# Group 0's FFN blocks on TensorE behind the spreads of C, its second tile's output ahead of the later gates, and its last tile's values and scale in the closing stage

## What is computed

```python
# x + xattn: hidden = ctx (4,256,128), z = layernorm(x) (4,256,256)
x = einsum(in_proj_w, hidden); xc = depthwise_conv(x, 4 taps); u = silu(xc + conv_b)
dt_lo, Bm, Cm = split(x_proj_w @ u)                    # 8, 16 and 16 rows
delta = softplus(dt_proj_w @ dt_lo + dt_proj_b); A = -exp(A_log)       # 256 x 16
state = state * exp(delta * A) + (delta * u) * B       # per token, per channel, 16 states
y = sum_over_16_states(state * C) + D * u;  y = y * silu(z)
x = x + y
# FFN on h = layernorm(x); bit_linear rounds x to 8 bits by its token's maximum and w to {-1,0,1}
gate = silu(bit_linear(h, gate_w, gate_b)); val = bit_linear(h, val_w, val_b)   # 1024 wide
x = x + bit_linear(gate * val, out_w, out_b)
```

## Time and profile before

| | |
|---|---|
| Median of 3 runs | 218.53 us (218.25 to 222.1) |
| The profiled execution | 218.7 us, of it the span from the first to the last instruction 216.8 us |
| Busy in the span | DVE 176.1 us, PE 149.0, POOL 137.5, ACT 133.4 |
| Mean granted clock of PE | 0.795 |
| The chain that ended last, by engine | DVE 22%, PE 21%, issue 8%, ACT 4%, POOL 2% |

### The profile page before, as it was taken

The page is one execution under the profiler, slowest core; times in us unless marked ns, Lnnn a source line. Parts: engine busy times, 40 slices in busy tenths (PEclk is TensorE's granted clock), DMA queues, the critical chain, the costliest instruction groups (busy, mean ns, idle before and its releaser), DMA issues.

```text
span 216.8 us, 2402 instructions
## 1 busy us (share of the span) xinstructions
PE 149.0 (69%) x706; PEld 92.4 (43%) x706; DVE 176.1 (81%) x269; ACT 133.4 (62%) x207; POOL 137.5 (63%) x134
## 2 busy tenths in 40 slices
PE   6983049871793687776107987737886478899983
PEld 5531035351451575566105444425463165335452
DVE  3787999959939969999999397996489998757771
ACT  2569656896189869761307579365975206286672
POOL 5039499997965994967849999993069004690000
PEclk9995558996555579696755587966699969999999
DMA  4994953450331110040024031322000000000002
GB/s 117 243 336 135 331 177 82 146 206 29 142 98 48 33 63 0 12 136 2 0 91 151 3 87 78 126 89 80 0 5 26 0 0 0 4 23 15 9 24 73
DMA packets 12689, 17.44 MB, mean 80 GB/s; under 512 B 3468, under 2 KB 9012, under 8 KB 12678
## 3 DMA queue, kind: packets, MB, share of 16 engines
q1 hardware_dynamic: 12678, 17.30, 24.9%
HBM read 16.11 MB, written 1.19 MB: 80 GB/s over the span
## 4 chain that ended last, share of the span: by engine, by line
DVE 22%; PE 21%; issue 8%; ACT 4%; POOL 2%; DVEq 0%; POOLq 0%
DVE state L934 4%; PE work L1275 4%; PE ysum L1189 4%; DVE wstate L944 3%; DVE gam L1015 2%; DVE xhat L849 2%; PE decay L1099 2%; DVE pool_state L934 2%; PE work L1099 2%; PE work L1282 2%; DVE wstage L1010 2%; PE work L1315 2%; PE decay L1275 1%; ACT gT L748 1%; PE cwide L1210 1%
## 5 line engine op out<-in xcount | busy, mean ns | idle before, releaser
L497 POOL TENSOR_TENSOR drive<-du,b_wide 128x1024 f32<-128x1024 f32 x31 | 73.8, 2395 | 3.1 <-DVE du L925 2.8
L679 ACT ACTIVATE decay<-delta,aneg 128x510 f32<-128x510 f32 x64 | 43.0, 685 | 29.5 <-DVE state L934 15.0
L934 DVE TENSOR_TENSOR_SCAN state<-decay,drive 128x512 f32<-128x512 f32 x44 | 52.4, 1208 | 2.7 <-ACT decay L679 2.4
L1189 PE MATMUL ysum<-ident,wstate 128*128 128x128 f32 x176 | 34.3, 343 | 9.8 <-DVE wstate L944 9.8
L1189 PEld LDWEIGHTS ysum<-ident,wstate 128*128 128x128 f32 x176 | 27.9, 180 | 18.0 <-DVE wstate L944 13.0
L944 DVE TENSOR_TENSOR wstate<-state,cwide 128x512 f32<-128x512 f32 x44 | 29.0, 662 | 7.5 <-issue 7.5
L507 POOL TENSOR_TENSOR pool_wstate<-pool_state,c_wide 128x1024 f32<-128x1024 f32 x10 | 23.6, 2361 | 13.7 <-PE ysum L1189 11.6
L1210 PE MATMUL cwide<-cparts,sel 128*128 128x512 bf16 x22 | 10.5, 476 | 26.0 <-DVE wstate L944 14.2
L934 DVE TENSOR_TENSOR_SCAN pool_state<-decay,drive 128x512 f32<-128x512 f32 x20 | 24.3, 1216 | 2.2 <-ACT decay L679 2.2
L1275 PE MATMUL work<-ternary,qT 128*128 128x512 bf16 x46 | 15.1, 416 | 3.8 <-ACT wstage L729 1.6
L1099 PE MATMUL work<-ident,wstage 128*128 128x128 f32 x80 | 12.5, 301 | 5.4 <-ACT ternary L703 2.8
(11 more groups left out here) (186 smaller groups left out, 290.5 us busy)
## 6 DMA issues: line engine op xcount, KB each, us to landing
b_wide<-bc_rows SPq DMA_DIRECT2D x16, 512.0 KB, 4.3
c_wide<-bc_rows SPq DMA_DIRECT2D x10, 256.0 KB, 3.4
x_in<-in_x SPq DMA_DIRECT2D x2, 512.0 KB, 4.0
wstage<-in_L_ffn_gate_w SPq DMA_DIRECT2D x1, 1024.0 KB, 7.6
wstage<-in_L_ffn_val_w SPq DMA_DIRECT2D x1, 1024.0 KB, 10.1
wstage<-in_L_ffn_out_w SPq DMA_DIRECT2D x1, 1024.0 KB, 8.9
ctx_in<-in_ctx SPq DMA_DIRECT2D x2, 256.0 KB, 3.7
out<-wtap SPq DMA_DIRECT2D x4, 128.0 KB, 1.7
```

Of the source, the lines that this page charges most:

```text
L497: nc.gpsimd.tensor_tensor(drive[:, m % NDR], du[:, m // NS], rows.unsqueeze(1).to_broadcast([P, EH, W]), ALU.mult).then_inc(s_drive, 1)
L679: nc.scalar.activation(v[:, :, 1:L], d[:, :, 1:L], ACT.Exp, scale=aneg[:, eh, n:n + 1]).then_inc(s_decay, 1)
L934: nc.vector.tensor_tensor_scan(dst, decay[i % ND][:], drive[:, i // EH % NDR, i % EH], 0.0, ALU.mult, ALU.add).then_inc(s_scan, 1)
L1189: last = nc.tensor.matmul(ysum[:, k, eh * P:(eh + 1) * P], lhsT=src[:, k * P:(k + 1) * P], rhs=ident[:], start=start and k % LB == 0, stop ...
```

## The change

It is made in the tables and in four places of the code. On PE, group 0's gate, val, turn and output blocks stand after other units than before; the z transposes move from unit 51 to 62. DVE and ACT follow. The output of tile 1 is formed before the gates of tiles 2 and 3. On DVE, the values and the scale of tile 3 leave the loop and come in the closing stage, behind the read of out02; ACT quantises that tile behind its gate(1, 0). POOL's scale parts for the second half of group 1 wait until tile 3's values are read. The list `scans` is written in the new order.

```diff
-PE_Z, ACT_Z, PE_ZLATE = (22, 23), (24, 25, 54, 55), 51
+PE_Z, ACT_Z, PE_ZLATE = (22, 23), (24, 25, 64, 65), 62
...
-PE_GATE, ACT_GATE = (39, 44, 51, 53), (44, 47, 56, 58)
-PE_VAL, DVE_VAL, DVE_VAL2 = (45, 48, 59, 60), (46, 48, 60, 62), (47, 49, 61, 62)
-ACT_QUANT, PE_TURN, ACT_TURN = (52, 54, 65, 68), (49, 54, 65), (53, 61, 67)
-PE_OUT, DVE_OUT = (50, 58, 67), (51, 60)
+PE_GATE, ACT_GATE = (40, 44, 56, 58), (44, 47, 58, 60)
+PE_VAL, DVE_VAL, DVE_VAL2 = (48, 50, 60, 67), (49, 51, 61), (50, 52, 62)
+ACT_QUANT, PE_TURN, ACT_TURN = (53, 55, 65), (52, 54, 65), (54, 57, 67)
+PE_OUT, DVE_OUT = (53, 55, 67), (54, 57)
...
-    scans += tile(0, 0, "val") + tile(0, 1, "val") + tile(0, 0, "turn", "out") + ["z2", "z3"]
-    scans += tile(0, 2, "gate") + tile(0, 3, "gate") + tile(0, 1, "turn", "out")
-    scans += tile(0, 2, "val") + tile(0, 3, "val") + tile(0, 2, "turn", "out")
+    scans += tile(0, 0, "val") + tile(0, 1, "val") + tile(0, 0, "turn", "out") + tile(0, 1, "turn", "out")
+    scans += tile(0, 2, "gate") + tile(0, 3, "gate") + tile(0, 2, "val") + ["z2", "z3"] + tile(0, 2, "turn", "out")
+    scans += tile(0, 3, "val")
...
                 if g:
                     wait_read(pool, "acol00")
+                if k:
+                    wait_read(pool, f"val0{GT - 1}{CH - 1}")
                 pool.wait_ge(s_tok, g + k + 1)
...
-            for i in range(ACT_QUANT[-1] + 1):
+            for i in range(ACT_TURN[-1] + 1):
                 if i < G * UNITS:
                     decays(i)
...
             for t in range(GT):
                 ffn_gate(1, t, ACT.Silu)
                 if t == 0:
+                    ffn_quantise(0, GT - 1)
                     ffn_hidden(0, GT - 1)
...
             ffn_output(0, GT - 2)
+            for c in range(CH):
+                ffn_value(0, GT - 1, c)
+            ffn_scale(0, GT - 1)
             for t in range(GT):
                 for c in range(CH):
                     ffn_value(1, t, c)
```

## The result

| | before | after |
|---|---|---|
| Median of 4 runs each | 219.63 us (218.25 to 222.1) | 227.0 us (225.83 to 227.78) |
| Ratio after / before, 95% interval | | 1.035 (1.026 to 1.045) |
| The profiled execution, and its span | 218.7, 216.8 | 226.95, 225.0 |
| Mean granted clock of PE | 0.795 | 0.780 |

The changed kernel is slower by 3.5%. The ratio compares the runs within 1.5% of the fastest of their kernel, the others being slow executions (of before here 222.1), so it is not the quotient of the medians. The next two rows are from the page of the profile of after: the busy time of each engine in the span, and the chain of work that ended last, by line.

What follows compares the result with a forecast made beforehand. DVE was taken as busiest, with PE bounding the end from 187.36. From 218.7, minus 3.4 (scans), plus 9.3 (val product) and 1.6 (turn), gave 226.2, median 226.0 us; 80% range 221.5 to 230.0.

Steps and rivals of the forecast that it cites:

- What bounds the end of the kernel: Closing stage: from 187.36, first half of group 1, PE is busy 21.27 of 21.40 us, so its delays reach the end.
- The first spread: Scans, unit 40: spread ahead of the gate block, weigh 3.1 us sooner, all of it going into waiting for POOL.
- Scan 48: Scans: ACT's block starts about 1.1 us sooner, so this scan starts at 134.7 instead of 137.34.
- waits (a) and (b): New DVE waits: 1.2 us at scan 59 (work0 held by out01), 2.7 us for decay 61 (ACT's second silu block).
- R: Start of the closing stage, 179.58 before; claimed 3.4 us sooner, bounds 0.5 to 5.5.
- Tile 3's val product: Closing stage: val031 waits for DVE's read of out02, holding up PE; delay 9.3 us, bounds 6.8 to 12.1.
- The clock term: Closing stage, PE after its stand: 5 us of half clock, costing 2.5 us of the delay.
- The turn: Closing stage: tile 3's transposition waits for ACT's quantising behind gate(1,0); 1.6 us on PE, 1.2 to 1.7.
- The one in which PE is hardly held: Rival, closing stage: out02 is read before PE reaches val031; 217.7 us, no change; chance 4%.
- The one with a cheap hold: Rival: PE is held as said, but cheaply, and the scans gain all; 221.0 us; chance 9%.
- The one in which the scans gain nothing: Rival: PE stays at half clock in the scans and gate 3 is late; 228.9 us, up to 231; chance 20%.
- The one in which the scans gain all that the two waits promise: Rival: the scans gain 7.4 us and PE is hardly held in the closing stage; 213.7 us; chance 2%.

Runs made afterwards that it cites:

- four experiments on the closing stage: Changed kernel with out02 read early, 218.48 us; or with out02 in bank 6 and a later turn, 216.49; also 14 warm-ups, 216.44; also POOL's additions later, 214.5.
- Re-ordering alone: Changed kernel with tile 3's val product, values, scale and quantising left in the scans; 218.78 us, ratio 0.997 to the kernel before.
- two experiments on out02: Changed kernel with out02 moved to bank 6, 222.88 us, ratio 1.006; or with DVE reading out02 ahead of normalising, 218.48 us, ratio 0.990.
- tail part alone: Kernel before with only tile 3's values, scale and quantising moved to the closing stage, its val product behind out02; 231.9 us, no ratio given.
- First spread alone: Kernel before with only tile 0's gate product on PE put behind the spread of unit 40; 217.22 us, ratio 0.993.

## Why the prediction was right, point by point

- **What bounds the end of the kernel.** "From 187.36 on the end of the kernel follows PE": right. In before, after and the four experiments on the closing stage in which PE's clock stays up, the time from the first half to the end is 29.3 to 31.1 us, wherever the first half lies.
- **The first spread.** Said: the weigh of unit 40 waits 0.6, then waits for POOL before scans 44 and 46, nothing won. Measured: 0.50, 1.34 and 1.71. The step held for the wait. "Buys nothing by itself" did not hold for the kernel: alone, the edit gave 0.7%, through stretches that I had taken as unchanged.
- **Scan 48, and waits (a) and (b).** Said 134.7, 1.2 and 2.7; measured 135.12, 1.19 and 2.62. All of after is 0.88 us later by scan 39 already (116.01 for 115.13), so scan 48 came some 0.5 us sooner than worked out. The wait before it, 1.55, is the shorter of its two lengths ("Re-ordering alone"): with the lower clock at that place it would have been 3.0 to 3.1, which the prediction did not see.
- **R.** Said 3.4 us sooner, with 1.2 us taken off for a low clock; measured 3.22 sooner, or 4.10 from scan 39 on. The wait for the last sum grew from 0.75 to 1.39 us: the sums stand behind the z transposes, and from 166.1 to 172.9 the granted clock was 0.50. That is a piece of the 1.2. That 3.22 lies so near to 3.4 is in part luck: the stretch that the prediction is about gained 4.10, 0.7 more than said, and the 0.88 us by which this execution was late before it took that back.
- **Tile 3's val product.** This is the step that makes the kernel slower. Said: a gap of some 5.8 us ended by the read of out02, val031 at R + 9.2, a delay of 9.3. Measured: 5.53 us ended by DVE's L1028, R + 9.21, 17.52 - 7.78 = 9.74. The two experiments on out02 show that this bank is the cause: 8.6 and 7.5 us of the delay go with it.
- **The clock term.** Said 2.5; val031 and the warm-ups took from 185.57 to 193.88, 8.31 us against 5.34 at full clock, so 3.0. That 0.5 is the miss in the delay: 5 us of half clock were taken, and 3.0 us lost stand for some 6. The choice of 5 between two rows was an estimate that no run bore out beforehand. The row that shows the level is that of 185 to 190, 0.50. The Trainium skill (TensorE: Matmul & The Clock Gate, Part 1) has the array at 1.2 GHz after idling. This trace agrees, with a granted clock of 0.50 behind the stand of 5.53 us. The same part of the Trainium skill puts the cost of ramping back at under 1% of a typical kernel's span, which would be at most 2.2 us here (an estimate). The trace shows 3.0 us, 1.3% of the span, for a single gap, and the measurement decides.
- **The turn.** Said 1.6; first half to end grew from 29.44 to 31.12, 1.7. The mechanism, ACT's quantising behind gate(1,0), is shown by the kernel that takes the turn later. Tile 3's values and scale cost nothing, as said: DVE is done with them at 190.0 and then waits 8.46 us. What the prediction did not have is that the turn's gap of 1.9 us can cost more than itself; in after it did not.
- **Sum.** -3.2 + 9.7 + 1.7 = +8.2, as the spans say (225.0 - 216.8); said were -3.4 + 9.3 + 1.6 = +7.5. The errors of +0.2, +0.4 and +0.1 have one sign, and 226.95 stands where 226.2 was worked out. By lengths from scan 39 on they have not: -0.7 in the scans, with 0.9 us from ahead of unit 39, then +0.4 and +0.1.
- **The rivals.** The one in which PE is hardly held is what happens once out02 has another bank or an early reader, and not otherwise. The one with a cheap hold fails on the clock: the hold cost 3.0 us at the lower level. The one in which the scans gain nothing fails on the 4.10 us. The one in which the scans gain all that the two waits promise is refuted by the re-ordering alone, with a ratio of 0.997.

## What to carry to other kernels

When a product is moved to a new place in a rotation of PSUM banks, look up what held its bank last, which engine reads that and behind how much other work: PE's queue stops at the first tile whose bank is not free, and everything behind it, fillers too, is late by the sum. A wait for one supplier is worth only as much as the next supplier is earlier; here two waits of 7.4 us in sum went, and five others of 1.2 to 2.6 us each, for POOL and ACT, came in their place, 8.4 us in sum. Matmuls put in to keep the clock up stood, before, where PE would have waited; when the queue ahead of them changes, as here, they turn in part from filler into cost.

## What the hardware showed

The clock did not always fall after a gap of the same length. The turn waits for 1.89 or 1.90 us in five kernels after almost the same work. In after and in the kernel with the early read the clock stays at 1.00 behind it (194 to 215 above, and 191 to 194 in the other); in the kernel with another bank and in that without warm-ups it falls (0.53 from 193 to 196 in the first, 0.50 from 194 to 196 in the second), and in the first that costs 1.5 us. A much longer spell shows in the profile of the tail part alone (231.59 us), busy times by stretch:

```profile
201.00:211.10 10.10, 10.10 (x31) 3.56 (x28) 4.92 (x13) 4.24 (x8) 0.00 (x0) 0.50 0.01 2
```

PE was busy for all of 10.10 us and yet stayed at the lower level, which made its first half to end 35.62 us instead of some 31. Nothing of the change is explained by that run. The prediction had priced the clock for the stand of nearly 6 us alone. What decides between falling and not falling at the short gap could not be told apart here; closing the gap was the cure: with it gone the clock is 1.00 from 186 to 208, and the ratio to before is 0.989 instead of 1.006. The same holds for the scans, where the clock at one place decided 1.5 us of a wait ("Re-ordering alone") and at another 1.6 us ("First spread alone").
